# First routed layer: row sums in pieces, and a constant operand of the one-hots moved to PSUM

## The reference

```
scores = softmax(xt @ Wr)                      # xt: 2048 x 128, 8 experts
G, idx = top_k(scores.T, k)                    # k = 512 tokens for each expert
X_in = xt[idx]
h = gelu(einsum('ekd,edh->ekh', X_in, W1) + b1)
X_e = einsum('ekh,ehd->ekd', h, W2) + b2
out = zeros.at[idx].add(G * X_e)               # several experts may hit one token
...
x = x + mixer0(xn) + routed0(xn)
xn = layernorm(x)
x = x + mixer1(xn) + routed1(xn)
```

## Time and profile before

| | us |
|---|---|
| median of 3 runs | 676.08 |
| lowest, highest | 675.97, 677.68 |
| profiled execution, whole | 682.82 |
| its span, from the first to the last instruction | 680.8 |

### The profile page before, as it was taken

How to read it: one execution, slowest core, us unless ns; L and a number is a source line. 1 busy time by engine, 2 the same in 40 slices (tenths; PEclk the granted TensorE clock), 3 DMA queues, 4 the chain that set the end, 5 groups by cost and what they waited for, 6 DMA issues and landing times.

```text
span 680.8 us, 12938 instructions
## 1 busy us (share of the span) xinstructions
PE 554.6 (81%) x3471; PEld 415.6 (61%) x3472; DVE 508.7 (75%) x1205; ACT 337.9 (50%) x809; POOL 444.9 (65%) x539
## 2 busy tenths in 40 slices
PE   3598986879899989989949889970576999999990
PEld 2433334657676757666638657760444778999990
DVE  7647677999999989998999751264776666666664
ACT  1655767737576656564724234420474554444430
POOL 3205592888999999998994687777026652555450
PEclk9999997979999999999979789995587979999996
DMA  7999000010000000000300244466941121222206
GB/s 241 173 284 286 0 6 0 1 63 1 1 1 0 0 0 0 0 0 0 122 6 17 61 115 127 145 222 185 368 162 45 45 61 43 58 55 58 57 24 185
DMA packets 55017, 54.83 MB, mean 81 GB/s; under 512 B 7743, under 2 KB 44182, under 8 KB 53952
## 3 DMA queue, kind: packets, MB, share of 16 engines
q1 hardware_dynamic: 49584, 42.57, 20.9%
q0 software_dynamic: 5392, 11.76, 6.8%
HBM read 34.24 MB, written 21.12 MB: 81 GB/s over the span
## 4 chain that ended last, share of the span: by engine, by line
PE 49%; DVE 24%; issue 8%; POOL 7%; ACT 6%; DMA 4%; DVEq 1%; SPq 1%; ACTq 0%; POOLq 0%
DVE arena L507 7%; PE bank L1050 7%; PE bank L1414 6%; PE bank L1401 6%; PE bank L1052 5%; POOL expert_rows L1926 4%; PE bank L1009 4%; PE bank L1093 2%; POOL bd L1858 2%; PE bank L977 2%; DVE arena L470 2%; PE bank L1018 2%; PE bank L1037 2%; DMA xnw<-expert_rows 1%; PE bank L1256 1%
## 5 line engine op out<-in xcount | busy, mean ns | idle before, releaser
L507 DVE TENSOR_TENSOR_SCAN arena<-bank,arena 128x256 f32<-128x256 f32 x256 | 160.9, 667 | 9.6 <-issue 7.5
L1548 ACT ACTIVATE arena<-delta,nega 128x256 f32<-128x256 f32 (+1 forms) x256 | 108.0, 499 | 8.8 <-DVE delta L428 7.0
L1874 POOL TENSOR_TENSOR arena<-arena 128x256 f32<-128x256 f32 x116 | 89.0, 771 | 26.2 <-DVE arena L470 21.7
L1050 PE MATMUL bank<-bd,xnw 128*128 128x258 f32 x256 | 86.0, 419 | 21.8 <-DVE arena L507 17.5
L1976 POOL DMA_INDIRECT pair_rows<-w1b,xnT x48 | 50.4, 1051 | 59.2 <-DVE w1b L766 50.5
L470 DVE SCALAR_TENSOR_TENSOR arena<-arena,inva,bank 128x256 f32<-128x256 f32 x192 | 82.5, 455 | 0.1
L1849 POOL TENSOR_TENSOR bd<-cfs,btok 128x258 f32<-128x258 f32 x128 | 79.4, 640 | 0.0
L1052 PE MATMUL bank<-bd,xnw 128*128 128x256 f32 x256 | 79.1, 391 | 0.0
L1050 PEld LDWEIGHTS bank<-bd,xnw 128*128 128x128 f32 x256 | 45.0, 196 | 46.1 <-DVE arena L507 25.2
L1009 PE MATMUL bank<-arena,ident 128*128 128x256 f32 x232 | 72.0, 393 | 0.9 <-DVEq L483 0.3
L1531 ACT ACTIVATE hbuf<-bank,inva 128x256 f32<-128x256 f32 x64 | 26.8, 469 | 84.5 <-PE bank L1037 84.3
(11 more groups left out here) (293 smaller groups left out, 1120.7 us busy)
## 6 DMA issues: line engine op xcount, KB each, us to landing
expert_rows<-bd SPq DMA_DIRECT2D x8, 1024.0 KB, 9.7
xnT<-expert_rows SPq DMA_DIRECT2D x4, 1024.0 KB, 5.0
bd<-in_w SPq DMA_DIRECT2D x4, 1024.0 KB, 13.4
arena<-in_w SPq DMA_DIRECT2D x4, 1024.0 KB, 14.6
slots_in<-bd POOLq DMA_DIRECT2D x1, 3120.0 KB, 25.1
xnT<-slots_in SPq DMA_DIRECT2D x48, 65.0 KB
xnw<-expert_rows SPq DMA_DIRECT2D x3, 1024.0 KB
bd<-in_w SPq DMA_DIRECT2D x8, 256.0 KB, 4.1
```

What stands on the lines that cost most here:

```text
L507: m = V.tensor_tensor_scan(zb[:, s % 8, r, :], dw_bank(par, s)[:, r * L:(r + 1) * L], abar[:, s % 8, r, :], 0.0, ALU.add, ALU.mult)
L1050: pe.matmul(o[:, :, 0:P + 1], xT[:, par, 0, h * P:(h + 1) * P], bd[:, par, 0, 2 * n2:2 * n2 + 2, :], start=True, stop=False, skip_group_ch ...
L1548: m = nc.scalar.activation(abar[:, s % 8, r, :], delta[:, h, bass.ds(b * L, L)], ACT.Exp, scale=negs[:, h, n:n + 1])
L1874: nc.gpsimd.tensor_tensor(zb[:, s % 8, 0, :], zb[:, s % 8, 0, :], zb[:, s % 8, 1, :], ALU.add).then_inc(S["q_ready"], 1)
```

## The change

Two edits, both on VectorE.

The row sum over 2048 columns becomes four sums over 512 columns, with no wait between them and one wait behind the last. And a copy of the row of numbers is put into bank 7, columns 128 to 255, behind the last step of the mixer; one-hots of experts 3 to 7 read that copy in place of `iota_p`. Their other operand, `place`, stays in SBUF. One-hots 0 to 2 read `iota_p` as before, since bank 7 is in use for the mixer until then.

```
+            iota_ps = bank[7][:, P:2 * P]
+
             def one_hot(e):
 
-                V.tensor_tensor(hot[e], iota_p[:, None, :].broadcast_to([P, NT, P]),
+                V.tensor_tensor(hot[e], (iota_ps if e > 2 else iota_p)[:, None, :].broadcast_to([P, NT, P]),
                                 place[:, :, e:e + 1].broadcast_to([P, NT, P]), ALU.is_equal).then_inc(S["hot_ready"], 1)
...
             mult(7, 15)
             finish(7, 1)
             dve.sem_inc(S["dve_done"], 1)
+            link(V.tensor_copy(iota_ps, iota_p))
             one_hot(3)
...
             def row_sum(e):
 
                 dve.wait_ge(S[f"rows_in{e % 2}"], 16 * (e // 2 + 1))
-                link(V.tensor_tensor(acc[:, :, :], acc[:, :, :], staged[e % 2], ALU.add))
+                for t in range(0, NT, 4):
+                    link.more(V.tensor_tensor(acc[:, t:t + 4, :], acc[:, t:t + 4, :], staged[e % 2][:, t:t + 4, :], ALU.add))
+                dve.wait_ge(S["dve_link"], link.n)
                 dve.sem_inc(S["row_sum"], 1)
```

## The result

The changed kernel takes 669.72 us (median of four runs, 668.52 to 670.34); the kernel before, timed beside it, takes 676.84 us (four runs, 675.97 to 677.68). The medians differ by 7.1 us; the ratio, which is not formed from the medians, is 0.9881, 95% interval 0.9844 to 0.9918. The change is faster, clear of noise. The profiled execution takes 670.34 us, span 668.4.

The account below looks back on a forecast made before the run. GpSimd's indirect DMAs, stalled by VectorE's two-SBUF instructions, were taken as the bound. Expert 7's load at 465.0 instead of 472.99 gave 8.0 us, 676.08 - 8.0 = 668.1 us; range 665.8 to 672.5, the forecast's own 666.3 to 670.0.

Parts of the forecast that it names:

- put 0: Sign on GpSimd: the first put of the first routed layer starts at 409 to 411 us, 6.7 us earlier.
- load 7: Load of expert 7's rows, ending the first routed layer's stage: issued at 465.0 instead of 472.99 us, sign 464 to 466.
- The port: GpSimd's indirect DMAs stall on VectorE instructions with two SBUF tensors, 15.6 us together; a PSUM operand or pieces free them.
- It is not the 15.6 us, since something else is late next.: First routed layer: the gain is 8.0 us, less than GpSimd's 15.6 us of stalls, as TensorE's data come later.
- TensorE does not move: First routed layer: TensorE's last two down products still end at 451.27 and 454.95 us.
- The path behind TensorE's end: From the last down products through gating, puts 6 and 7 and landing: 454.95 to expert 7's load at 465.0 us.
- Gating 6 was to follow its down product at once: VectorE's gating of expert 6: done at 452.8 us after its down product at 451.27, put 6 starting at 453.1.
- rival B: Puts fall into the 1 MB loads: load 7 1.8 us late, another 1 us lost, 670.9 us; chance 0.10.
- Stalls left in the last eight puts: Puts 6 and 7 on GpSimd: row sums 4 and 5 and gating 7 still cost 0.7 us (0 to 1.8).
- Landing of put 7: From GpSimd's end of put 7 to the load of expert 7's rows: 1.29 us.
- Nothing is lost behind load 7: After 473 us every step hangs on this load, so the gain goes to the end; clock costed at zero, +-1 us.
- rival D: The stage gains 8 us, the next gives half back through TensorE's clock staying low longer: 672 us; chance 0.04.

Follow-up runs that it names:

- e9_eight: The changed kernel with row sums in eight pieces of 256 columns instead of four of 512; 696.63 us, ratio to the kernel before 0.9984 (0.9957 to 1.0011).
- e5_before: The kernel before itself, nothing changed, profiled on chip b in a later session; 694.52 us in one run, beside 699.41 us for that session.
- e1_onehots: The kernel before with only one-hots 3 to 7 reading the row of numbers from PSUM, row sums whole; 696.44 us, ratio 0.9984 (0.9951 to 1.0018).

## Why the prediction was right, and where it was not

The forecast was 668.1 us (-8.0); measured were 669.72 (-7.1). The mechanism on GpSimd came as predicted. Three terms behind TensorE's end were too small by 3.2 us together, the frame that the sum stood in was off by an execution's low clock, and the two errors partly cancel. Three of the named signs missed with the frame: put 0 (405.04 for 409 to 411), TensorE's last down product (448.56 for 455) and load 7 (461.81 for 464 to 466).

- *The port.* Right. Bank operand: every gather 0.94 to 0.98 from 385 to 415 us (mean 947 ns), put 0 at 405.04 where I had 409.8 less the 4.7 us by which the queue started earlier. Pieces: 2.50 us against 2.55 expected, no put over 1.50, and e9_eight shows the scaling. One-hot 2.29 as taken, copy 0.29 against 0.3, and hidden, though by less than I took: the 1.39 us of waiting that cover it in the earlier trace rows are 0.39 at full clock (e5_before), and the first gather of expert 3 starts 6.1 us behind the mixer's end with the copy and without.
- *"It is not the 15.6 us, since something else is late next."* Right: 11.6 us left GpSimd's instructions and 5.1 came back as waits and landing.
- *"TensorE does not move."* Right of the change, wrong of the two traces. Its last down product ended at 454.95 before and 448.56 after. Of these 6.4 us, 2.3 are the mixer's end, and four groups at the lower clock level in the profile of before alone are 4.1 (1.64 against 1.10 us, 3.68 against 1.97, 1.06 against 0.60, 5.03 against 3.68). So of the 11.2 us between the two loads only 4.8 came behind TensorE's end, where the forecast had all its 8.0. It took a profile with low clock spells as the typical one, and found "no reason for the stage to differ" between that profile and the timed runs, which are 6 us shorter. Set by GpSimd's queue, 83.20 us from its own start, the load of before would stand at 385.06 + 83.20 = 468.3 in an execution like that of after, 6.4 us behind 461.81 and near the measured 7.1. That is an estimate. By the same frame the forecast's own path would have put load 7 at 448.56 + 10.05 = 458.6, a gain of 9.7; the terms below take 3.2 of it back. That 8.0 fell within 0.9 us of the 7.1 is in part luck.
- *The path behind TensorE's end.* Here the sum was 3.2 us short: load 7 follows TensorE's end by 461.81 - 448.56 = 13.25 us, and I had 465.0 - 454.95 = 10.05. Three terms:
  - Gating 6 was to follow its down product at once. That ended near 441.25 + 3.66 = 444.9, put 6 was due 1.8 us behind it, at 446.7, and started at 448.25: 1.5 us late, held by row sum 3 as the chain shows. Load 2 (issued 429.38) and put 3's last piece (430.58) overlapped, and the put took 6.99 us to land; that the load was the reason is argued from the overlap, no run tests it. This is of rival B's kind, at 1.5 us instead of 2.8, in a place that the forecast's margins of "1 to 2 us" left out, since they began with put 4.
  - Stalls left in the last eight puts, those of experts 6 and 7: 1.6 instead of 0.7 (11.5 us against 10.6).
  - Landing of put 7: 2.05 instead of 1.29.
- *Nothing is lost behind load 7.* Right: 207.8 us before, 206.6 after; rival D did not come.
- *The range.* It held the time. But it was drawn as if the gain were the kernel's alone: the same kernel gained 2.4 and 3.8 us and then nothing (0.8 slower) in three later sessions by the medians, 1.4, 2.7 and -0.3 by the ratios, and only the second of these intervals excludes no change.

What the experiments show is the mechanism: which edit shortens which DMA, and by how much. That it is worth 7 us rests on the result and its two traces alone. The share of rival B under the conditions of the result stays open too, since every experiment ran under others.

## What to carry to other kernels

Where a GpSimd DMA ends a constant time after a VectorE instruction, look at that instruction's operands: one constant in PSUM frees GpSimd inside it, and cutting an instruction with two SBUF tensors to 512 columns bounds the stall at some 0.5 us for 0.2 us of VectorE's time. Then count the gain at the next engine, from the start of the queue that is the bound and not from an end that a low clock may have moved. And time such a change on more than one chip, and compare the clock of two traces before comparing places in them. In the later sessions here signals of TensorE came late beside runs of back-to-back indirect DMAs, and shorter DMAs came back in part as waits.

## What the runs showed of the hardware

- A constant read from a bank leaves the duration of a 2048-column VectorE comparison as it was (2.28 us from SBUF, 2.28 to 2.29 with the bank), and gathers inside it take 0.94 us instead of up to 2.94.
- Between VectorE instructions that follow one another without a gap GpSimd gets its turn: the longest put is 3.05 us beside whole row sums (e1_onehots), 1.50 beside 512-column pieces and 1.24 beside 256-column ones (e9_eight).
- A put that starts 1.2 us after a 1 MB load takes 6.99 us from its start to its landing (after, 430.58); put 7 took 2.24 before and 3.00 after.
- In every session but the result's, some signals of TensorE to VectorE and ScalarE (the 55 "remote" waits) arrived late, 52 of them 0.9 to 3.1 us behind the end of an unbroken run of GpSimd's indirect DMAs and up to 9 us after the matmuls that they stand for; lengthening one run by 5.0 us moved its signal by 5.1. There the same kernel takes 21 to 23 us more, and from load 7 to the end 220 to 224 us instead of 207, with more "remote" waits in the second layer.
- One kernel's traces differ in TensorE's clock behind the mixer: 0.50 or 1.00 in 385 to 388 us, worth 2.4 us from the mixer's end to the next gather.
